# A two-layer attention and expert kernel on one core: where the linear stage makes its low halves, its decays and its first sum

## The reference

```python
x = _layernorm(x + _L0_attn_ref(x, ...))    # 16 heads, window of 16 to both sides
x = _layernorm(x + _L0_ffn_ref(x, ...))     # 16 experts, top 4
x = _layernorm(x + _L1_attn_ref(x, ...))    # linear attention with decay
x = _layernorm(x + _L1_ffn_ref(x, ...))     # 8 experts, top 2
```

## Time and profile before

| | us |
|---|---|
| runs | 983.86, 987.30, 991.93 |
| median | 987.3 |
| profiled execution | 991.68 |
| its span in the profile | 989.8 |
| mean granted TensorE clock, of full speed | 0.87 |

### The profile page before, as it was taken

The page is one execution under the profiler, slowest core; times in us unless marked ns, Lnnn a source line. Parts: engine busy times, 40 slices in busy tenths (PEclk is TensorE's granted clock), DMA queues, the critical chain, the costliest instruction groups (busy, mean ns, idle before and its releaser), DMA issues.

```text
span 989.8 us, 35004 instructions
## 1 busy us (share of the span) xinstructions
PE 733.4 (74%) x11638; PEld 598.6 (60%) x11639; DVE 661.4 (67%) x1902; ACT 523.6 (53%) x1305; POOL 529.9 (54%) x546
## 2 busy tenths in 40 slices
PE   3889888788987119999999981746765199999900
PEld 0566666566666118999999880635544089898900
DVE  4357678577667408777777773678885367777756
ACT  2456565455554117677676764544431167777723
POOL 2013468358665746777776771276656534444433
PEclk9799999899997559999999995777677599999955
DMA  7011122112122236444444534322210233222153
GB/s 211 13 46 34 47 62 72 44 58 72 54 66 61 94 99 101 106 107 100 114 101 110 117 69 139 105 84 83 81 44 29 81 64 66 65 55 60 43 174 91
DMA packets 136221, 79.71 MB, mean 81 GB/s; under 512 B 104386, under 2 KB 116841, under 8 KB 136128
## 3 DMA queue, kind: packets, MB, share of 16 engines
q1 hardware_dynamic: 122240, 51.76, 22.0%
q0 software_dynamic: 13312, 25.31, 8.1%
q10 hardware_dynamic: 576, 1.34, 0.4%
HBM read 33.12 MB, written 32.63 MB: 66 GB/s over the span
## 4 chain that ended last, share of the span: by engine, by line
PE 56%; DVE 19%; issue 11%; POOL 7%; DMA 3%; ACT 3%; DVEq 0%; SPq 0%; POOLq 0%; ACTq 0%
PE avbank L1723 8%; PE proj L1723 7%; POOL xs L651 5%; PE avbank L1576 4%; PE s L1702 3%; PE s L1704 3%; PE s L1703 3%; PE t L1702 3%; PE t L1704 3%; PE t L1703 3%; DVE nm L804 2%; PE t L1563 2%; PE proj L1482 2%; DVE rden L824 2%; DVE yf L1047 2%
## 5 line engine op out<-in xcount | busy, mean ns | idle before, releaser
L714 POOL DMA_INDIRECT yt<-ysb,to_now x224 | 232.8, 1039 | 160.8 <-ACT ysb L1333 99.9
L651 POOL DMA_INDIRECT xs<-x1p,sidx x192 | 190.7, 993 | 147.0 <-ACT prob L1252 57.5
L944 DVE CAST h_hi<-act_out 128x512 bf16<-128x512 f32 x152 | 65.1, 428 | 72.7 <-ACT act_out L1346 64.9
L1702 PE MATMUL s<-xt,w_hi 128*128 128x256 bf16 x296 | 81.8, 276 | 41.5 <-DMA xt<-xs 41.5
L945 DVE TENSOR_TENSOR h_lo<-act_out,h_hi 128x512 bf16<-128x512 f32 x152 | 105.5, 694 | 5.2
L1252 ACT ACTIVATE prob<-t 128x384 f32<-128x384 f32 (+1 forms) x160 | 73.0, 510 | 41.6 <-PE t L1563 41.5
L1723 PE MATMUL avbank<-w_hi,h_hi 128*128 x448 | 81.0, 220 | 2.0 <-issue 0.8
L1703 PE MATMUL s<-xt,w_hi 128*128 128x256 bf16 x296 | 81.9, 277 | 0.0
L1704 PE MATMUL s<-xt,w_lo 128*128 128x256 bf16 x296 | 81.9, 277 | 0.0
L1702 PE MATMUL t<-xt,w_hi 128*128 128x256 bf16 x296 | 81.3, 275 | 0.0
L1703 PE MATMUL t<-xt,w_hi 128*128 128x256 bf16 x296 | 81.1, 274 | 0.0
(11 more groups left out here) (230 smaller groups left out, 2082.4 us busy)
## 6 DMA issues: line engine op xcount, KB each, us to landing
w_raw<-w_all SPq DMA_DIRECT2D x59, 256.0 KB
gat<-yt SPq DMA_DIRECT2D x8, 1024.0 KB, 5.5
gat<-yt SPq DMA_DIRECT2D x8, 512.0 KB, 4.1
yt<-ysb,to_now POOLq DMA_INDIRECT x224
xs<-tail_rows SPq DMA_DIRECT2D x24, 129.0 KB, 2.6
xs<-x1p,sidx POOLq DMA_INDIRECT x192
out<-ow SPq DMA_DIRECT2D x8, 256.0 KB, 2.4
xt<-xs SPq DMA_TRANSPOSE x112
```

The costliest lines, as they stand in the source:

```text
L651: pool.indirect_dma_start(out=xs[n][:, :], out_offset=bass.IndirectOffsetOnAxis(sidx[:, par, at:at + 1], 0), in_=x1p[:, par, t, k, :], in_ ...
L714: pool.indirect_dma_start(out=yt[n][:, :], out_offset=bass.IndirectOffsetOnAxis(to_now[:, u, s:s + 1], 0), in_=ysb[:, u, s, :], in_offset= ...
L944: ch.link(dve.tensor_copy(h_hi[:, par, c, :], act_out[:, par, c, :]))
L1702: pe.matmul(dst, w_h, xt[:, u, 0, :], start=True, stop=False)
```

## The change

1. In POOL's `linear_body` the weights' low half is gone. Of the five left-over row groups three are sent before `low_rows`, two after it.
2. DVE makes the weights' low half at the end of its body (`late_weights`).
3. DVE does all four decays of the next batch ahead of `weigh`; decays 2 and 3 stood behind `place`.
4. PE does `ranks` before `write_values`, not after.
5. The first batch's expert results are summed by DVE alone, in sixteen instructions of 128x128 that multiply by the routing weight and add; ACT's `scale_results(0, 0, 0)` is gone, and `pair_up(b)` waits for one count less.
6. The clearing of the second `vf` buffer stands ahead of `split_half`.
7. ACT has one more tiny Exp behind L1427, at the build-up.

```diff
--- before.py
+++ after.py
@@ -669,11 +669,6 @@
                 pool.wait_ge(var3_ready, b + 1)
                 pool.tensor_tensor(rstd3[:, :], ve3[:, :], nhalf, ALU.pow).then_inc(rstd3_ready, 1)
 
-            def low_weights(b, par):
-                pool.wait_ge(hi_done, CHUNKS_0 + b + 1)
-                pool.tensor_tensor(w1_lo[:, bass.ds((GROUPS_0 + b) * CH, CH)], w_raw[:, par, :],
-                                   w1_hi[:, bass.ds((GROUPS_0 + b) * CH, CH)], ALU.subtract).then_inc(lo_done, 1)
-
             FIRST = 3
 
             def send_of(par, places):
@@ -684,9 +679,10 @@
 
                 rstd_of_y3(b)
                 if prev:
-                    send_of(1 - par, range(FIRST, T * K1))
+                    send_of(1 - par, range(FIRST, 2 * FIRST))
                 low_rows(1, b, par)
-                low_weights(b, par)
+                if prev:
+                    send_of(1 - par, range(2 * FIRST, T * K1))
                 pool.wait_ge(slots_ready[1], b + 1)
                 pool.wait_ge(x1_spread, B + b + 1)
                 apart(pool)
@@ -970,7 +966,7 @@
 
             def pair_up(b, par):
 
-                dve.wait_ge(weighted_in, b + 1)
+                dve.wait_ge(weighted_in, b)
                 ch.link(add(gat0[:, par, :, 0:2, :], gat0[:, par, :, 0:2, :], gat0[:, par, :, 2:4, :]))
 
             def add_up(b, par):
@@ -995,6 +991,13 @@
                 dve.wait_ge(ws_ready, T * b + e + 1)
                 dve.tensor_tensor(pm[e][:, :], ws_bank[e][:, 0:L - e * P],
                                   decay_m[:, 0:L - e * P], ALU.mult).then_inc(decayed, 1)
+
+            def late_weights(b, par):
+
+                at = (GROUPS_0 + b) * CH
+                dve.wait_ge(hi_done, CHUNKS_0 + b + 1)
+                dve.tensor_tensor(w1_lo[:, bass.ds(at, CH)], w_raw[:, par, :], w1_hi[:, bass.ds(at, CH)],
+                                  ALU.subtract).then_inc(lo_done, 1)
 
             def linear_body(b, i, par, prev, nxt, nxt2):
 
@@ -1024,16 +1027,14 @@
                 choose(1)
                 mark(1)
                 if nxt:
-                    decay_of(b + 1, 0)
-                    decay_of(b + 1, 1)
+                    for e in range(T):
+                        decay_of(b + 1, e)
                 weigh(1, b)
                 take_ranks(1, b, rank_ps)
                 place(1, b, par)
-                if nxt:
-                    decay_of(b + 1, 2)
-                    decay_of(b + 1, 3)
                 if nxt2:
                     y_stats()
+                late_weights(b, par)
 
             def final_sums(b):
 
@@ -1147,9 +1148,9 @@
             for s, half, parts in ((0, 0, slice(0, 2)), (0, 1, slice(2, 4)), (1, 0, slice(0, 3, 2)), (1, 1, slice(1, 4, 2))):
                 ins = dve.tensor_copy(spread_of[:, s, half, :, parts, :], bc(head_rows, 2, 2))
             ins.then_inc(spread_ready, 1)
+            dve.memset(vf[:, 1, :, :, :], 0.0).then_inc(v_zero, 1)
             split_half(0, 0)
             split_half(0, 1)
-            dve.memset(vf[:, 1, :, :, :], 0.0).then_inc(v_zero, 1)
             take_odd(0, 0, 1)
             dve.wait_ge(loaded_later, 16 * LOADS_LATER)
             prep_stats(1)
@@ -1193,8 +1194,15 @@
             dve.tensor_tensor(decay_m[:, :], decay_m[:, :], causal, ALU.mult).then_inc(decay_ready, 1)
             dve.wait_ge(decay_ready, 1)
             dve.wait_ge(x1_kept, B)
-            pair_up(0, 0)
-            add_up(0, 0)
+            dve.wait_ge(gathered[0][0], 16)
+            for k in range(K0):
+                for t in range(T):
+                    ins = dve.scalar_tensor_tensor(out=y[:, t, :], in0=gat0[:, 0, t, k, :], scalar=wres[:, t, k:k + 1],
+                                                   in1=y[:, t, :] if k else xres[:, t, :], op0=ALU.mult, op1=ALU.add)
+                if k < K0 - 1:
+                    ch.link(ins)
+            ins.then_inc(comb_done, 1)
+            dve.wait_ge(comb_done, 1)
             y_stats()
             x2_apply(0)
             pair_up(1, 1)
@@ -1425,6 +1433,7 @@
             nc.scalar.activation(dlog[:, :], dexp[:, :], ACT.Ln, bias=1.0).then_inc(dlog_ready, 1)
             act.wait_ge(wc_ready, 1)
             nc.scalar.activation(wc[:, :], avbank[:, 0:D], ACT.Identity, scale=alpha[:, 0:1])
+            nc.scalar.activation(decay_m[:, 0:1], ones_f[:, 0:1], ACT.Exp)
             act.wait_ge(masks_in, 16 * MASKS)
             lay_max(0, 0)
             over_attention(act, body)
@@ -1438,7 +1447,6 @@
             nc.scalar.activation(decay_m[:, :], nmat, ACT.Exp, scale=dlog[:, 0:1]).then_inc(expd_ready, 1)
             expert_tiles(0)
             act.wait_ge(init_done, 2)
-            scale_results(0, 0, 0)
             scale_results(1, 1, 0)
             keep_x2_turned(0)
             keep_values(0)
@@ -1793,8 +1801,9 @@
                 if nxt:
                     for e in range(1, T):
                         write_scores(b + 1, e)
+                ranks(1, b, rank_ps)
+                if nxt:
                     write_values(b + 1)
-                ranks(1, b, rank_ps)
 
             turn(0)
             pe.wait_ge(xn_ready, 1)
```

## The result

| | before | after |
|---|---|---|
| median, us | 988.2 (4 runs, 983.9 to 991.9) | 976.2 (4 runs, 973.0 to 977.1) |
| profiled execution | 991.68 | 976.83 |
| span | 989.8 | 975.0 |

The ratio is 0.9874, 95% interval 0.9827 to 0.9922: 12.0 us faster between the medians, where 11.1 were forecast from a median of 987.3. As a time, the interval is a gain of 7.7 to 17.1 us: it is clear of no change and wide. The profiled executions lie 14.85 apart, 2.9 more than the medians; the account further down says where.

A forecast was written before the change was run, and what follows sets the result against it. In the linear stage DVE, then GpSimd, were taken to end last, with PE beside them. Linear stage 7.3, first sum 2.9 and clearing 0.85 give 11.1 us off the median 987.3: 976.2 us, range 970 to 984.

The forecast's parts named there:

- Step 1: Linear cycle, GpSimd: low_rows follows three left-over scatters, ending 5.9 us after x1f; the two scatters left end at 8.3.
- Step 2: Linear cycle, DVE: dtop, a 128x8 subtraction, meets one scatter instead of two subtractions and ends at 7.1 us, not 9.3.
- Step 3: Linear cycle, DVE: four decays ahead of the weights wait for PE's scores, end at 9.8 us, taking back 1.1 of 2.2.
- Step 4: Linear cycle, DVE: the slots' end (sidx) moves from 13.1 to 12.0 us after x1f; ranks cost nothing.
- Step 5: Linear cycle, slots to next x1f: late weights cost GpSimd's scatters 0.2 us; cycle 18.7 against 19.68, 5.0 over five.
- Step 6: Linear cycle, PE: twenty read matmuls in one run, ending at 14.7 us at full clock, hidden by the 18.7 cycle.
- The last batch: Last linear batch: dtop falls from 2.05 to some 0.5 us, so eight scatters start 1.5 us earlier.
- The clearing: Build-up: memset moved into DVE's wait; copy starts 1.35 us earlier, but the constants' load leaves 0.85, bounds 0 and 1.35.
- the reads at a low clock: Rival, linear stage: clock stays low through PE's reads in all five cycles, cycle 20.0 us, total 982.8; chance 0.13.
- the rival of the early stage: Rival, build-up and first batch: the 3.75 us of first sum and clearing halve or go, total 979.9; chance 0.08.
- The rival of the ports: Rival, linear stage: each late weight holds a scatter up for its whole 0.68 us, total 979.1; chance 0.12.
- The slower case: Rival, linear stage: dtop stays as late as 9.3 us, the mask gates PE, cycle 20.5, total 989.9; chance 0.05.

The follow-up runs named there:

- experiment 5: Changed kernel with low_rows back behind all five left-over scatters, the weights still on DVE: cycle 19.04 us, one execution 980.6 us.
- experiment 4: Kernel before with one wait added, GpSimd holding low_rows and low_weights until the batch's mask is made: cycle 18.6 us, one execution 981.75 us.
- experiment 7: Changed kernel with decays 2 and 3 back behind the slots: ratio to before 0.9828, cycle 17.6 us.
- experiment 9: Changed kernel with the late weights' subtraction made twice on DVE, first into a spare buffer: mean cycle 18.37 us against 18.28.
- experiment 8: Changed kernel with decays 2 and 3 behind the slots and two row groups sent ahead instead of three: ratio to before 0.9781, median 967.1 us.
- experiment 1: Kernel before with only the clearing moved ahead of split_half: ratio 0.9993, not to be told from no change.
- experiment 3: Changed kernel with first sum, clearing and table load put back, leaving the linear stage's reordering alone: ratio to before 0.9910, 8.9 us.
- experiments 5 and 6: The second of the two: changed kernel with the weights' low half back on GpSimd behind low_rows, none on DVE: ratio to before 0.9861.

## Why the prediction was right

The forecast was 976.2 and the measured median 976.2. That the two agree to the tenth is luck. The gain between the medians was 12.0 and not 11.1, and the kernel before came out at 988.2 and not at the 987.3 that I had subtracted from: the two misses cancel, and both are small beside the interval of 7.7 to 17.1 us. The mechanism was right. The terms were less so: put together from the profiles they come to 13.1 us (9.7 in the linear stage, 2.9 for the sum, 0.5 for the clearing), where I had 11.05.

- *Step 1, low_rows in POOL's gap.* Right to 0.1 us: (4.8) to (5.9), then scatters from (6.1) to (8.3). Experiment 5 shows that this is the step that matters.
- *Step 2, dtop.* The direction was right and the size on the safe side: I let it wait for the scatter's end, (7.1). It ends at (6.8). The step behind it, that a scatter may hold dtop up, was wrong (experiment 4). It cost the forecast nothing, since step 3 absorbs it.
- *Step 3, the decays wait for PE.* Right: the second pair ends at (9.8), and the chain now runs through PE's scores. I took this as a price that comes with the change; experiment 7 shows that it needn't be paid.
- *Step 4, slots at (12.0).* (11.9) in the cycle shown, and (11.4) to (12.0) in the five.
- *Step 5, the ports' 0.2 and the cycle's 18.7.* Mis-sized. From sidx's end to the rstd it is 4.33, as before, with a price of 0.02 (experiment 9). That is half of the miss of 0.4 us a cycle. The other half is PE's clock: where it rises before the last scores, these and the slots come up to 0.6 earlier. In the third batch's cycle the four matmuls of the last two blocks took 0.82 us instead of 1.28, at a granted clock of 1.00, and the slots ended at (11.4). I had taken one cycle with PE at the lower level up to (9.5) for all five.
- *Step 6, the reads.* Right, and better than taken: they ended at (13.1) to (14.5), because the values were there earlier and all twenty went at full clock. In the cycle shown the statistics behind the reads are done at 713.44, and GpSimd comes to the second rstd at 714.41 only: hidden by 1.0. It isn't hidden by as much everywhere: in the sixth batch the reads ended at (14.5). Experiment 8 uncovers this side.
- *The last batch* gave 1.9 for 1.5, since the scatter beside dtop didn't hold it up: it took 0.17, where I had taken 0.5. The table behind the slots, put off by 0.58, was hidden by the scatters as said; these themselves ended 0.1 later.
- *The first sum* gave the 2.9 us of its working.
- *The clearing* was over-sized: 0.85, measured about half a microsecond over twelve profiles. The mechanism, a wait for the constants that takes the place of the copy's, was right: the wait is there in the changed kernel and in five others, though not in experiment 1. The landing, which I took from one execution, varies: in the changed kernel's own it came 1.4 later than I had it.
- *The early table load* gave nothing that can be seen, as said; it wasn't tested alone.

Of the rivals, the reads at a low clock did not come about. The sum over the linear stage was 7.3 and measured 9.7 in the profile, 8.9 by experiment 3; the early stage was 3.75, and measured 3.4 (2.9 and the clearing's 0.5), so the rival of the early stage fell too; in the profiled execution alone, with its late constants, it gave 2.3. The rival of the ports didn't come about either: the late weights cost a scatter 0.02, since they end just behind its start. The slower case, a mask later than (9.5), didn't: dtop ended at (6.8).

GpSimd's subtractions of two operands held dtop up to their own end, 0.02 to 0.03 us behind it, in experiments 5 and 6. The Trainium skill (SBUF — State Buffer, section "SBUF: two separate sides") says that the side that starts first has the shared ports for its whole instruction and the other is blocked. By those ends the trace agrees. By the recorded starts it doesn't, since dtop is recorded 0.38 us ahead of low_rows in experiment 5 and yet waits. In the other direction it agrees in that a scatter loses about what is left of DVE's subtraction (0.45 with 0.58 left, experiment 9); that a subtraction begun 0.05 us behind a scatter's start isn't held up at all doesn't follow from it.

## What to carry to other kernels

Where two engines share ports, look at what stands queued behind the running instruction on the other engine, not only at what is recorded as running: a big subtraction that isn't urgent should be put where the other engine has no two-operand work, and a single wait can be enough for it. When a stall goes, look again at everything that had been ordered around it: here two operations were moved ahead of the slots together with the repair, and putting them back, with one row group fewer sent ahead, gave another 9 us. A wait of one engine for another that a change adds is to be priced before the change is kept, however small the operations behind it.

## What was unexpected of the hardware

- *A GpSimd subtraction stops DVE before its own recorded start.* dtop was stopped by a GpSimd subtraction recorded as starting 0.39 us after it (kernel before) and 0.38 us after it (experiment 5), while the scatter ahead of that was still running. With the same scatter running, and no operation of two operands queued behind it, dtop took 0.17 us (changed kernel, experiment 4). In all four dtop began 0.53 to 0.60 us into the scatter, so it isn't the phase. Whether the subtraction takes the ports early, or its start is recorded late, the traces don't tell.
- *A split run of reads can fall to the low clock, an unsplit one did not.* In the four kernels whose reads wait for the late decays in the middle, the fourteen matmuls behind that wait ran slow in six of twenty cycles. Six and fourteen read matmuls of one such cycle, in experiment 1:

```profile
694.92 0.93 PE L1782 MATMUL proj<-vv,pm 128*128 128x128 f32 x6 [0.64 <-ACT vv L1390]
...
697.12 3.33 PE L1782 MATMUL proj<-vv,pm 128*128 128x128 f32 x14 [1.26 <-DVE pm L996]
```

  There the fourteen take 3.33 us at a granted clock of 0.53, after six at 1.00, and the cycle takes 20.5. In the eight kernels in which the reads run through, none of the forty cycles had this. By what the clock is decided was not looked into. A split doesn't always cost: in experiment 4 the reads were split too, by pauses of 0.06 to 0.54 us where the other three kernels had 0.72 to 1.77, and they ran at the upper level in all five cycles.
- *A scatter waits for what DVE has under way, not for what DVE begins beside it.* It takes 0.96 us alone, and 1.03 to 1.10 beside x1f's scalings, which isn't explained here. With a DVE operation of two SBUF operands of 128x512 or more under way at its start it takes longer, by what that one has left less some 0.13: 0.14 left, 0.98 (changed kernel); 0.58 left, 1.41 (experiment 9, first cycle); 0.64 left, 1.47 (L965's 1.21 us from 699.22, under the scatter at 699.79 of the changed kernel). Where one of the two operands lies in PSUM it costs nothing: with 0.58 us left of y3's sum from the reads' bank a scatter took 0.96 (at 656.39, changed kernel). A subtraction of 0.68 us begun 0.05 us behind the scatter's start costs it nothing and isn't itself lengthened (experiment 9). So what such an operation costs is set by its place to a tenth of a microsecond.
